# Four instead of two key tiles of the value product in parts, in five of eight chunks

## The chip, the cores and the metric

One core of a Trainium2 chip. The metric is the device time of one launch in microseconds (us), from the median of several runs. TensorE (PE) multiplies; VectorE (DVE), ScalarE (ACT) and GpSimd (POOL) work on vectors; SyncE (SP) issues the DMAs.

## What is computed

A transformer layer in fp32 on x of 4 x 1024 tokens x 256:

```
xn  = layernorm(x)
out = x + attention(xn) + ffn(xn)
attention: qkv = xn @ w_qkv, 16 heads of 128, rotary on q and k,
           softmax(q k^T / sqrt(128)) v, then @ w_out
ffn:       gelu(xn @ up + up_bias) @ down + down_bias, up and down in MXFP4 (blocks of 32)
```

## The kernel before

**Two ways to multiply fp32.** A product of plain fp32 operands is one call in the program and two matmul records in the trace. A product "in parts" splits both operands into a high part, rounded to the reduced type fp32r, and a low part (the value less its high part), and adds three reduced products: high x high, low x high, high x low. All products of the kernel are in parts, but for the value product (probabilities x v), which takes only the first two of its eight key tiles in parts (`SPLIT = 2`); the other six are plain fp32.

**Order of the work.** The 4 x 16 heads are taken as 32 pairs of heads. A pair has 8 chunks of 256 queries, 4 for each head; chunk number k mod 8 is called chunk 0 to 7 here. Each engine runs a function `step` once for each chunk, always in the same order, and the engines meet by semaphores. Two pairs are one round of 16 steps. The steps are in hardware loops whose body starts with step 4 of a round and ends with step 3 of the next (`PEELED = 4`), so that each engine jumps back between a step 3 and a step 4 in every second pair. The first eight pairs also split the projection weights.

**PE**, step k: scores of the next chunk's first 128 queries (`next_scores(0)`, L1222, into `s_ps`), a projection group of the next pair into `slot_ps`, scores of its second 128 queries, output projection of chunk k-2 (L1222, into `w_ps`), a second projection group, and last the value product of chunk k-1 (`values`, L1282 to L1306): L1296, L1297 and L1300 are the three products of each of the two tiles in parts, L1304 the six plain tiles. It waits for `p_hi_ready` ahead of L1296 and for `p_lo_ready` ahead of L1300.

At steps 3 and 7, `next_scores(0)` starts a new head, and waits first until all four rotated pieces of that head's q and k are there (`qk_ready`, L1273).

**DVE**, step k: transposes (L943) of the probabilities, from which the DMAs (L420) build `keys_first`, the probabilities with keys on the partitions; low part of the attention output (L963), row maxima (L933), output added to y (L974), and MXFP4 pieces.

**ACT**, step k: high part of the attention output of chunk k-2 (`high_out`, L767), copies of the projection groups out of PSUM (`take_group`; L722 for v, L735 to L737 for q and k), two exponentials (L755), the high part of a rotated piece (`rotated_high`, L747), and last the high part of the chunk's own probabilities (`probs_high`, L761): 128x512 elements of `keys_first` into `p_hi`, once its DMAs have landed.

**POOL**, step k, in this order: the low part of the probabilities of chunk k-1 (`probs_low`, L605, waits for L761), then the rotary work. A rotation (`rotated_sum`) is three operations, L584, L585 and L587. ACT then takes the high part (L747), and POOL the low part (`rotated_low`, L598), which raises `qk_ready`. The q and k pieces of the next pair's first head ("qk0", pieces 0 to 3) are rotated in steps 3, 4, 5 and 6; the low parts of pieces 0 and 1 come in steps 4 and 5 ahead of the next rotation, those of pieces 2 and 3 in step 6, around the last rotation. Those of the second head are rotated in steps 7, 0, 0 and 1. Step 0 is the one with two rotations.

In ACT's step k, `rotated_high` stands ahead of `probs_high`, and waits for POOL's rotation of the same step (in step 6 it stands ahead of the second exponential too).

The v projection comes in four groups of two key tiles; `V_TILES = (1, 2, 0, 3)` says which pair of tiles each holds. Only the group with tiles 0 and 1 (`V_SPLIT`) is split: high part by ACT (L722, `v_hi`), low part by DVE (L957, `v_lo`). The others are copied by ACT to `v_rows`. PE may write the PSUM bank again when that is done (`bank_free`).

Of the kernel before, what the change touches and what calls it, by code (L numbers as in the profile page):

```python
# [8 lines left out]
F32 = mybir.dt.float32  # L9
F32R = mybir.dt.float32r  # L10
U32 = mybir.dt.uint32
ACT = mybir.ActivationFunctionType
ALU = mybir.AluOpType
# [4 lines left out]
HEADS, HEAD = 16, 128  # L18
FF = 1024
P = 128  # L20
TOK = BATCH * SEQ
TILES = TOK // P
BT = SEQ // P
# [20 lines left out]
LN_STEP = TILES // ROUNDS  # L44
MX_HALF = MX_COLS // 2

SPLIT = 2


def layer(nc, d):  # L50
# [7 lines left out]
    with ExitStack() as ctx:  # L58
        def sb(name, shape, dt=F32):
            return ctx.enter_context(nc.sbuf_tensor(name, shape, dt))  # L60

        def sem(name):
            return ctx.enter_context(nc.semaphore(name))

        def pb(name, shape):
# [18 lines left out]

        qk_hi, qk_lo = seq_parts[:, 1], seq_parts[:, 2]

        v_rows = sb("v_rows", [P, 2, BT - SPLIT, 2 * HEAD])
        v_hi = sb("v_hi", [P, 2, SPLIT, 2 * HEAD], F32R)
        p_hi = seq_parts[:, 3, 0].rearrange("p c s -> p (c s)")[:, 0:2 * SPLIT * CHUNK].rearrange(
            "p (s a j q) -> p s a j q", s=2, a=2 * QUADS, j=SPLIT)  # L90
# [9 lines left out]
        keys_first = sb("keys_first", [P, 2, 2 * QUADS, BT, QUAD], F32R)  # L100
# [75 lines left out]
        v_ready = sem("v_ready")  # L176
        v_lo_ready = sem("v_lo_ready")
        p_hi_ready = sem("p_hi_ready")
        p_lo_ready = sem("p_lo_ready")
        scores_ready = sem("scores_ready")  # L180
        max_ready = sem("max_ready")
        probs_ready = sem("probs_ready")
# [59 lines left out]

        V_TILES = (1, 2, 0, 3)
        V_SPLIT = tuple(n for n in range(4) if V_TILES[n] < SPLIT // 2)

        USED = {"qk0": 5, "v": 12, "qk1": 11}

# [13 lines left out]
        def qk_number(part, n):  # L261

            return n + (4 if part == "qk1" else 0)
# [312 lines left out]
        def _(pool):  # L576
# [23 lines left out]
            def probs_low(c, k):  # L600

                slot = k % 2
                pool.wait_ge(p_hi_ready, c + 1)
                low = keys_first[:, slot, :, 0:SPLIT, :]
                nc.gpsimd.tensor_tensor(low, low.bitcast(F32), p_hi[:, slot, :, :, :].bitcast(F32),  # L605
                                        ALU.subtract).then_inc(p_lo_ready, 1)

            def w_low(p, part):

# [87 lines left out]
        def _(act):  # L697
# [17 lines left out]
            def take_group(p, place, part, n, parity, bank, first=False):  # L715


                act.wait_ge(proj_ready, p * 12 + place + 1)
                if part == "v":
                    at = 2 * V_TILES[n]  # L720
                    rows = v_hi[:, parity, at:at + 2, :] if n in V_SPLIT else v_rows[:, parity, at - SPLIT:at - SPLIT + 2, :]
                    nc.scalar.activation(rows, bank.rearrange("p (a b) -> p a b", a=2), ACT.Copy).then_inc(v_ready, 1)  # L722
                    return
                m = qk_number(part, n)

                if first and m == 4:
                    act.wait_ge(first_qk_dve, 1)
                elif first and m == 5:
                    act.wait_ge(first_qk_dve, 3)
                elif not (first and m < 4):  # L730
                    act.wait_ge(qk_ready, p * 8 + m - 1)
                scale = SCALE if n // 2 == 1 else 1.0
                a, b = rope_slot(p, m)
                h = HEAD // 2
                nc.scalar.activation(a, bank, ACT.Copy, scale=scale)  # L735
                nc.scalar.activation(b[0:h], bank[h:P], ACT.Copy, scale=scale)
                nc.scalar.activation(b[h:P], bank[0:h], ACT.Copy, scale=scale).then_inc(rope_in, 1)  # L737
# [20 lines left out]
            def probs_high(i, k):  # L758

                act.wait_ge(keys_moved[k % 4], chunk_moves(i, k))  # L760
                nc.scalar.activation(p_hi[:, k % 2], keys_first[:, k % 2, :, 0:SPLIT, :].bitcast(F32),  # L761
                                     ACT.Copy).then_inc(p_hi_ready, 1)

            def high_out(c, slot):
# [453 lines left out]
        def _(pe):  # L1218
# [63 lines left out]
            def values(i, k, first):  # L1282

                c, p = i * 16 + k, i * 2 + k // 8
                pe.wait_ge(keys_moved[k % 4], chunk_moves(i, k))
                if not (first and k == 0):
                    pe.wait_ge(o_lo_ready, c)
                if k % 8 == 0:
                    pe.wait_ge(v_ready, p * 4 + 3)
                    pe.wait_ge(v_lo_ready, (p + 1) * len(V_SPLIT))  # L1290
                parity, head, slot = (k // 8) % 2, (k // 4) % 2, k % 2
                cols = slice(head * HEAD, (head + 1) * HEAD)
                out = o_ps[:, 0:CHUNK]
                pe.wait_ge(p_hi_ready, c + 1)
                for kt in range(SPLIT):
                    nc.tensor.matmul(out, v_hi[:, parity, kt, cols], p_hi[:, slot, :, kt, :], start=(kt == 0), stop=False)  # L1296
                    nc.tensor.matmul(out, v_lo[:, parity, kt, cols], p_hi[:, slot, :, kt, :], start=False, stop=False)  # L1297
                pe.wait_ge(p_lo_ready, c + 1)
                for kt in range(SPLIT):
                    nc.tensor.matmul(out, v_hi[:, parity, kt, cols], keys_first[:, slot, :, kt, :], start=False, stop=False)  # L1300
                if k % 8 == 0:
                    pe.wait_ge(v_ready, p * 4 + 4)
                for kt in range(SPLIT, BT):
                    last = nc.tensor.matmul(out, v_rows[:, parity, kt - SPLIT, cols], keys_first[:, slot, :, kt, :].bitcast(F32),  # L1304
                                            start=False, stop=(kt == BT - 1))
                last.then_inc(o_ready, 1)  # L1306

# [94 lines left out]
            def step(i, k, first, last):  # L1402
                c = i * 16 + k
                t = c * 2
                tail = last and k >= 16

                def next_scores(n):
                    if last and k == 15:
                        return
                    k2 = 2 * k + 2 + n  # L1410
                    pe.wait_ge(probs_ready, t + n + 1)
                    scores(k2, i * 2 + k2 // 16, k2 % 8 == 0 or (first and k2 == 4))

                def slot(n):
                    bank = slot_ps[:, n]
                    if (k, n) == LN_SLOT:
                        bank_free(i, k, n, first, last)
                        pe.wait_ge(ln_xn_ready, i + 3)
                        for m in range(CT * LN_STEP):
                            ins = nc.tensor.transpose(bank[:, m * P:(m + 1) * P],  # L1420
                                                      ln_xn[:, m % LN_STEP, (m // LN_STEP) * P:(m // LN_STEP + 1) * P], ident[:, :])
                        ins.then_inc(ln_turned, 1)
                        return
                    if (k, n) == MX_SLOT:
                        bank_free(i, k, n, first, last)
                        pe.wait_ge(mx_ready, i + 1)
                        for m in range(MX_STEP // P):
                            ins = nc.tensor.transpose(bank[:, m * P:(m + 1) * P], mx_q[:, m * P:(m + 1) * P], ident[:, :])
                        ins.then_inc(mx_turned_ready, 1)
                        return  # L1430
                    g = group_at(k, n, last)
                    if not g:
                        return
                    place, part, num, ahead = g
                    if first and k == 0:
                        if n == 0:
                            pe.wait_ge(v_ready, 1)
                        else:
                            pe.wait_ge(rope_in, 6)
                    else:  # L1440
                        bank_free(i, k, n, first, last)
                    if num == 0:
                        pe.wait_ge(w_ready[part], (i * 2 + ahead + 1) * 16)
                    if place < 2 and ahead == 2:
                        pe.wait_ge(x_ready[place], ((i + 1) // 4 + 1) * 32)
                    project(part, num, bank)

                if tail:
                    up(0, 0, k - 16)
                else:  # L1450
                    next_scores(0)
                    slot(0)
                    next_scores(1)
                if not (first and k < 2):
                    output(c - 2, (k - 2) % 16, i * 2 + (k - 2) // 8, first and k == 2)
                if not tail:
                    slot(1)
                if not (first and k == 0) and not (last and k == 17):
                    values(i, k - 1, first)
# [74 lines left out]
```

## Time and profile before

| | |
|---|---|
| Median of 3 runs | 2454.54 us (2453.13 to 2455.77) |
| The profiled execution | 2453.68 us |
| Its span, first to last instruction | 2451.9 us |
| Busy: PE, DVE, ACT, POOL | 2417.3, 1920.8, 1678.6, 1731.7 us |
| Mean granted TensorE clock | 0.999 |

A busy share is that of the whole span. Matmul records overlap: the time that one takes of the engine is the distance from its start to the next one's start, not its duration. In the tables a waiting instruction's idle time is named with what ended it.

### The profile page before, as it was taken

The numbers are of one execution on the slowest core, as the hardware profiler recorded it, in microseconds if no ns is written. First come the engines' busy times: TensorE is split into PE (matmuls) and PEld (weight loads), VectorE is DVE, ScalarE is ACT, GpSimd is POOL, SyncE is SP. The second block draws the span as 40 slices with busy tenths as digits, with TensorE's granted clock in tenths as the row PEclk, the third lists the DMA queues.
The fourth block names the chain that finished last, engine by engine and source line by source line (L and its number), as shares of the span: only waits on it lengthen the run. The fifth ranks groups of instructions, "written<-read, shape, count | busy, mean of one in ns | idle before, by whom it ended". The sixth has DMA issues, their size and how long they took to land. (4 is left out here: it accounts for less than half of the span.)

```text
span 2451.9 us, 42811 instructions
## 1 busy us (share of the span) xinstructions
PE 2417.3 (99%) x13168; PEld 2123.8 (87%) x13168; DVE 1920.8 (78%) x2671; ACT 1678.6 (68%) x3039; POOL 1731.7 (71%) x1358
## 2 busy tenths in 40 slices
PE   6999999999999999999999999999999999999999
PEld 5888888888888888888888888888888888888798
DVE  7878888787877877787787778778777877777776
ACT  7777777776776777676677767667776766777433
POOL 4778877777777777777677777777777777777331
PEclk9999999999999999999999999999999999999999
DMA  4666666667666656667666666667676666656832
GB/s 143 181 170 167 169 158 177 158 167 195 183 161 150 156 148 162 156 151 195 180 159 147 164 154 152 162 149 190 158 183 156 151 162 149 156 146 171 240 132 69
DMA packets 400878, 396.72 MB, mean 162 GB/s; under 512 B 38656, under 2 KB 383104, under 8 KB 400768
## 3 DMA queue, kind: packets, MB, share of 16 engines
q1 hardware_dynamic: 400768, 395.67, 62.9%
q14 instruction: 91, 0.75, 0.1%
q8 instruction: 19, 0.31, 0.1%
HBM read 91.43 MB, written 35.65 MB: 52 GB/s over the span
## 5 line engine op out<-in xcount | busy, mean ns | idle before, releaser
L933 DVE TENSOR_REDUCE neg_max<-s_ps 128x1 f32<-128x1024 f32 x512 | 621.1, 1219 | 289.1 <-PE s_ps L1222 288.2
L1222 PE MATMUL s_ps<-seq_parts 128*128 128x512 f32 x3072 | 826.3, 408 | 1.3 <-DVE seq_parts L1097 0.8
L755 ACT ACTIVATE probs<-s_ps,neg_max 128x1024 f32<-128x1024 f32 x512 | 571.1, 1115 | 369.0 <-DVE neg_max L933 365.3
L1304 PE MATMUL o_ps<-keys_first,v_rows 128*128 128x256 f32 x3072 | 706.5, 380 | 1.3 <-ACT v_rows L722 1.3
L943 DVE STREAM_TRANSPOSE turned_blocks<-probs 128x1024 f32<-128x1024 f32 x512 | 630.6, 1237 | 61.3 <-ACT probs L755 38.8
L1222 PEld LDWEIGHTS s_ps<-seq_parts 128*128 128x128 f32 x3072 | 571.5, 188 | 116.9 <-ACT probs L755 1.4
L1304 PEld LDWEIGHTS o_ps<-keys_first,v_rows 128*128 128x128 f32 x3072 | 566.3, 190 | 68.1 <-ACT v_rows L722 1.5
L605 POOL TENSOR_TENSOR keys_first<-keys_first,seq_parts 128x512 fp32r<-128x512 f32 x256 | 333.0, 1301 | 318.1 <-ACT seq_parts L761 318.0
L584 POOL TENSOR_TENSOR rope_a<-rope_a,cos 128x512 f32<-128x512 f32 x252 | 325.7, 1292 | 178.8 <-ACT rope_b L737 178.6
L598 POOL TENSOR_TENSOR seq_parts<-rope_a,seq_parts 128x512 fp32r<-128x512 f32 x252 | 360.2, 1430 | 92.8 <-ACT seq_parts L747 92.8
L1222 PE MATMUL slot_ps<-seq_parts,w_parts 128*128 128x512 f32 x1506 | 387.9, 393 | 0.0
L587 POOL TENSOR_TENSOR rope_a<-rope_a,rope_b 128x512 f32<-128x512 f32 x252 | 326.0, 1294 | 19.8
L585 POOL TENSOR_TENSOR rope_b<-rope_b,sin 128x512 f32<-128x512 f32 x252 | 326.7, 1297 | 0.0
L1222 PEld LDWEIGHTS slot_ps<-seq_parts,w_parts 128*128 128x128 f32 x1506 | 272.9, 189 | 51.7 <-ACT rope_b L737 0.5
L747 ACT ACTIVATE seq_parts<-rope_a 128x512 fp32r<-128x512 f32 x252 | 222.1, 881 | 80.4 <-POOL rope_a L587 79.9
L974 DVE SCALAR_TENSOR_TENSOR y<-w_ps,inv_sum,y 128x256 f32<-128x256 f32 x512 | 224.4, 480 | 33.5 <-DVE inv_sum L951 7.8
L767 ACT ACTIVATE o_hi<-o_ps 128x256 fp32r<-128x256 f32 x256 | 98.0, 383 | 165.5 <-PE o_ps L1304 141.9
L1222 PEld LDWEIGHTS slot_ps<-w_parts,seq_parts 128*128 128x128 f32 x1524 | 197.5, 189 | 9.1 <-issue 0.9
L1222 PE MATMUL slot_ps<-w_parts,seq_parts 128*128 128x256 f32 x1524 | 203.1, 283 | 0.5 <-ACT rope_b L737 0.5
L1222 PEld LDWEIGHTS w_ps<-wo_parts,o_hi 128*128 128x128 f32 x1024 | 175.1, 190 | 29.5 <-DVE o_lo L963 9.1
L1222 PE MATMUL w_ps<-wo_parts,o_hi 128*128 128x256 f32 x1024 | 194.3, 282 | 6.4 <-DVE o_lo L963 6.3
L761 ACT ACTIVATE seq_parts<-keys_first 128x512 fp32r<-128x512 f32 x256 | 159.7, 624 | 59.3 <-DMA keys_first<-turned_blocks 57.8
(118 smaller groups left out, 2606.8 us busy)
## 6 DMA issues: line engine op xcount, KB each, us to landing
keys_first<-turned_blocks SPq DMA_DIRECT2D x2048, 128.0 KB, 2.7
w_parts<-w_qkv_parts SPq DMA_DIRECT2D x72, 512.0 KB, 4.2
w_qkv_parts<-w_parts SPq DMA_DIRECT2D x24, 512.0 KB, 3.7
wo_parts<-w_out_parts SPq DMA_DIRECT2D x48, 256.0 KB, 3.2
seq_parts<-xnt_parts SPq DMA_DIRECT2D x16, 512.0 KB, 4.4
w_raw<-in_w_qkv SPq DMA_DIRECT2D x24, 256.0 KB, 4.1
seq_parts<-xnt_parts SPq DMA_DIRECT2D x6, 1024.0 KB, 8.3
y<-in_x SPq DMA_DIRECT2D x16, 256.0 KB, 3.2
```

The source lines that it names most:

```text
L584: nc.gpsimd.tensor_tensor(a, a, cos[:, cols], ALU.mult).then_inc(rope_mult, 1)
L585: nc.gpsimd.tensor_tensor(b, b, sin[:, cols], ALU.mult).then_inc(rope_mult, 1)
L587: nc.gpsimd.tensor_tensor(a, a, b, ALU.add).then_inc(rope_sum, 1)
L598: nc.gpsimd.tensor_tensor(lo, total, hi.bitcast(F32), ALU.subtract).then_inc(qk_ready, 1)
L605: nc.gpsimd.tensor_tensor(low, low.bitcast(F32), p_hi[:, slot, :, :, :].bitcast(F32), ALU.subtract).then_inc(p_lo_ready, 1)
L747: nc.scalar.activation(hi, total, ACT.Copy).then_inc(rope_hi, 1)
L755: nc.scalar.activation(probs[:, k2 % 4, :], s_ps[k2 % 2][:, :], ACT.Exp, bias=neg_max[:, col:col + 1], accum_out=row_sum[:, col:col + 1]). ...
L933: nc.vector.tensor_reduce(neg_max[:, k2 % 16:k2 % 16 + 1], s_ps[k2 % 2][:, :], AXX, ALU.max, negate=True).then_inc(max_ready, 1)
L943: nc.vector.transpose(turned_blocks[:, k % 2, n].rearrange("p b j q -> p j b q"), probs[:, (2 * k + n) % 4, :].rearrange("p (j b q) -> p j ...
L974: last = nc.vector.scalar_tensor_tensor(rows, w_ps[:, n * DIM:(n + 1) * DIM], inv_sum[:, col:col + 1], rows, ALU.mult, ALU.add)
L1222: ins = nc.tensor.matmul(out, w, m, start=(n == 0), stop=(n == len(terms) - 1))
L1304: last = nc.tensor.matmul(out, v_rows[:, parity, kt - SPLIT, cols], keys_first[:, slot, :, kt, :].bitcast(F32), start=False, stop=(kt == B ...
```

## The change

Chunks 2 to 6 of each pair (`WIDE`) take four key tiles in parts, the others two as before (`NARROW`). In a wide chunk ACT's L761 takes 128x1024 elements, POOL does a second subtraction of 128x512 behind the first (a semaphore of its own, `p_lo_back`), and PE does 12 products in parts and 4 plain tiles. PE waits for both low parts ahead of the first product that reads one. Of v, tiles 2 and 3 (group 0) are now kept both ways: ACT copies the group to `v_rows` and then rounds it into `v_hi`, DVE makes its `v_lo`, and PE may write the bank again only after that. The order of the steps is otherwise the same.

```
+NARROW, SPLIT = 2, 4
+WIDE = (2, 3, 4, 5, 6)
...
+        V_COPIED = tuple(n for n in range(4) if V_TILES[n] >= NARROW // 2)
+        FRONT, BACK = slice(0, NARROW), slice(NARROW, SPLIT)
...
 probs_low (POOL)
-                low = keys_first[:, slot, :, 0:SPLIT, :]
-                nc.gpsimd.tensor_tensor(low, low.bitcast(F32), p_hi[:, slot, :, :, :].bitcast(F32),
-                                        ALU.subtract).then_inc(p_lo_ready, 1)
+                low = keys_first[:, slot, :, FRONT, :]
+                nc.gpsimd.tensor_tensor(low, low.bitcast(F32), p_hi[:, slot, :, FRONT, :].bitcast(F32),
+                                        ALU.subtract).then_inc(p_lo_front, 1)
+                if k % 8 in WIDE:
+                    low = keys_first[:, slot, :, BACK, :]
+                    nc.gpsimd.tensor_tensor(low, low.bitcast(F32), p_hi[:, slot, :, BACK, :].bitcast(F32),
+                                            ALU.subtract).then_inc(p_lo_back, 1)
...
 take_group (ACT)
+                    tiles = bank.rearrange("p (a b) -> p a b", a=2)
+                    if n in V_COPIED:
+                        ins = nc.scalar.activation(v_rows[:, parity, at - NARROW:at - NARROW + 2, :], tiles, ACT.Copy)
+                    if n in V_SPLIT:
+                        ins = nc.scalar.activation(v_hi[:, parity, at:at + 2, :], tiles, ACT.Copy)
+                    ins.then_inc(v_ready, 1)
...
 probs_high (ACT)
+                tiles = slice(0, SPLIT if k % 8 in WIDE else NARROW)
+                nc.scalar.activation(p_hi[:, k % 2, :, tiles, :], keys_first[:, k % 2, :, tiles, :].bitcast(F32),
                                      ACT.Copy).then_inc(p_hi_ready, 1)
...
 values (PE)
+                wide = k % 8 in WIDE
+                tiles = SPLIT if wide else NARROW
-                for kt in range(SPLIT):
+                for kt in range(tiles):
                     (high x high and low x high)
-                pe.wait_ge(p_lo_ready, c + 1)
+                pe.wait_ge(p_lo_front, c + 1)
+                if wide:
+                    pe.wait_ge(p_lo_back, wide_chunks(p, k))
+                for kt in range(tiles):
                     (high x low)
...
+                for kt in range(tiles, BT):
                     (plain fp32)
```

## Rows read from the trace of the kernel before

**Rows 1.** The page: busy time of each engine (share).
```profile
PE 2417.3 (99%) x13168; PEld 2123.8 (87%) x13168; DVE 1920.8 (78%) x2671; ACT 1678.6 (68%) x3039; POOL 1731.7 (71%) x1358
```
**Rows 2.** Waits: waiting engine and line, releaser, total us, times, longest.
```profile
ACT seq_parts L747 <- POOL rope_a L587: 79.9, 64, 2.0
...
PE o_ps L1300 <- POOL keys_first L605: 3.8, 2, 3.1
```
**Rows 3.** Timeline, PE, 1317 to 1321 us: start, us, line, operands, count.
```profile
1317.13 0.28 PE L1296 MATMUL o_ps<-seq_parts,v_hi 128*128 128x256 f32 x1
...
1317.85 2.75 PE L1304 MATMUL o_ps<-keys_first,v_rows 128*128 128x256 f32 x12
1320.25 1.73 PE L1222 MATMUL s_ps<-seq_parts 128*128 128x512 f32 x6
```
**Rows 4.** Timeline, POOL, 1285 to 1323 us: steps 3 to 7 of one pair.
```profile
1287.06 1.29 POOL L584 TENSOR_TENSOR rope_a<-rope_a,cos 128x512 f32<-128x512 f32 x1 [1.12 <-ACT rope_b L737]
...
1298.32 1.30 POOL L587 TENSOR_TENSOR rope_a<-rope_a,rope_b 128x512 f32<-128x512 f32 x1
...
1306.84 1.29 POOL L587 TENSOR_TENSOR rope_a<-rope_a,rope_b 128x512 f32<-128x512 f32 x1
1310.55 1.29 POOL L605 TENSOR_TENSOR keys_first<-keys_first,seq_parts 128x512 fp32r<-128x512 f32 x1 [2.42 <-ACT seq_parts L761]
1311.80 1.30 POOL L598 TENSOR_TENSOR seq_parts<-rope_a,seq_parts 128x512 fp32r<-128x512 f32 x1
...
1315.69 1.29 POOL L587 TENSOR_TENSOR rope_a<-rope_a,rope_b 128x512 f32<-128x512 f32 x1
1317.72 1.28 POOL L598 TENSOR_TENSOR seq_parts<-rope_a,seq_parts 128x512 fp32r<-128x512 f32 x1 [0.74 <-ACT seq_parts L747]
...
1322.80 1.30 POOL L584 TENSOR_TENSOR rope_a<-rope_a,cos 128x512 f32<-128x512 f32 x1 [2.19 <-ACT rope_b L737]
```
**Rows 5.** Timeline, ACT, 1283 to 1318 us: steps 2 to 6 of the same pair.
```profile
1283.93 0.63 ACT L761 ACTIVATE seq_parts<-keys_first 128x512 fp32r<-128x512 f32 x1 [1.11 <-DMA keys_first<-turned_blocks]
...
1291.00 1.14 ACT L747 ACTIVATE seq_parts<-rope_a 128x512 fp32r<-128x512 f32 x1 [0.87 <-POOL rope_a L587]
...
1299.75 1.14 ACT L747 ACTIVATE seq_parts<-rope_a 128x512 fp32r<-128x512 f32 x1
1309.34 0.62 ACT L747 ACTIVATE seq_parts<-rope_a 128x512 fp32r<-128x512 f32 x1
...
1317.01 0.63 ACT L747 ACTIVATE seq_parts<-rope_a 128x512 fp32r<-128x512 f32 x1 [1.65 <-POOL rope_a L587]
```
**Rows 6.** Timeline, all engines, 1223 to 1249 us: a pair with the jump back.
```profile
1223.91 0.39 ACT L767 ACTIVATE o_hi<-o_ps 128x256 fp32r<-128x256 f32 x1 [2.75 <-issue]
...
1246.86 1.27 POOL L598 TENSOR_TENSOR seq_parts<-rope_a,seq_parts 128x512 fp32r<-128x512 f32 x1 [0.74 <-ACT seq_parts L747]
...
1248.97 0.81 PE L1222 MATMUL s_ps<-seq_parts 128*128 128x512 f32 x2
```
**Rows 7.** Groups by shape, ACT and DVE: count | busy us, mean ns.
```profile
L761 ACT ACTIVATE seq_parts<-keys_first 128x512 fp32r<-128x512 f32 x256 | 159.7, 624 | 59.3 <-DMA keys_first<-turned_blocks 57.8
L767 ACT ACTIVATE o_hi<-o_ps 128x256 fp32r<-128x256 f32 x256 | 98.0, 383 | 165.5 <-PE o_ps L1304 141.9 <-issue 22.9
L722 ACT ACTIVATE v_rows<-slot_ps 128x512 f32<-128x512 f32 x96 | 56.5, 590 | 0.0
L957 DVE TENSOR_TENSOR seq_parts<-slot_ps,v_hi 128x512 fp32r<-128x512 f32 x31 | 21.1, 681 | 0.0
```
**Rows 8.** Timeline, PE, 52 to 58 us, the start of the kernel.
```profile
52.30 0.50 PE L1300 MATMUL o_ps<-keys_first,v_hi 128*128 128x256 f32 x2 [3.13 <-POOL keys_first L605]
54.06 4.24 PE L1304 MATMUL o_ps<-keys_first,v_rows 128*128 128x256 f32 x12 [1.26 <-ACT v_rows L722]
57.95 3.08 PE L1222 MATMUL s_ps<-seq_parts 128*128 128x512 f32 x12
```
**Rows 9.** Stretches: us, busy and count of PE, PEld, DVE, ACT, POOL, clock.
```profile
55.00:56.00 1.00, 1.00 (x4) 0.74 (x3) 0.00 (x0) 0.98 (x3) 0.87 (x1) 0.50 0.10 33
```

More of the change, by code:

```diff
@@ L45 @@
 MX_HALF = MX_COLS // 2
-SPLIT = 2
+NARROW, SPLIT = 2, 4
+WIDE = (2, 3, 4, 5, 6)
 def layer(nc, d):
@@ L85, in layer @@
         qk_hi, qk_lo = seq_parts[:, 1], seq_parts[:, 2]
-        v_rows = sb("v_rows", [P, 2, BT - SPLIT, 2 * HEAD])
+        v_rows = sb("v_rows", [P, 2, BT - NARROW, 2 * HEAD])
         v_hi = sb("v_hi", [P, 2, SPLIT, 2 * HEAD], F32R)
@@ L178, in layer @@
         p_hi_ready = sem("p_hi_ready")
-        p_lo_ready = sem("p_lo_ready")
+        p_lo_front = sem("p_lo_front")
+        p_lo_back = sem("p_lo_back")
         scores_ready = sem("scores_ready")
@@ L244, in layer, with wide_chunks @@
         V_SPLIT = tuple(n for n in range(4) if V_TILES[n] < SPLIT // 2)
+        V_COPIED = tuple(n for n in range(4) if V_TILES[n] >= NARROW // 2)
+        FRONT, BACK = slice(0, NARROW), slice(NARROW, SPLIT)
+        def wide_chunks(p, k):
+            return p * len(WIDE) + WIDE.index(k % 8) + 1
         USED = {"qk0": 5, "v": 12, "qk1": 11}
@@ L720, in take_group @@
                     at = 2 * V_TILES[n]
-                    rows = v_hi[:, parity, at:at + 2, :] if n in V_SPLIT else v_rows[:, parity, at - SPLIT:at - SPLIT + 2, :]
-                    nc.scalar.activation(rows, bank.rearrange("p (a b) -> p a b", a=2), ACT.Copy).then_inc(v_ready, 1)
+                    tiles = bank.rearrange("p (a b) -> p a b", a=2)
[4 more added lines that the diff above has]
+                    ins.then_inc(v_ready, 1)
                     return
@@ L760, in probs_high @@
                 act.wait_ge(keys_moved[k % 4], chunk_moves(i, k))
-                nc.scalar.activation(p_hi[:, k % 2], keys_first[:, k % 2, :, 0:SPLIT, :].bitcast(F32),
+                tiles = slice(0, SPLIT if k % 8 in WIDE else NARROW)
+                nc.scalar.activation(p_hi[:, k % 2, :, tiles, :], keys_first[:, k % 2, :, tiles, :].bitcast(F32),
                                      ACT.Copy).then_inc(p_hi_ready, 1)
@@ L1294, in values @@
                 pe.wait_ge(p_hi_ready, c + 1)
-                for kt in range(SPLIT):
+                wide = k % 8 in WIDE
+                tiles = SPLIT if wide else NARROW
+                for kt in range(tiles):
                     nc.tensor.matmul(out, v_hi[:, parity, kt, cols], p_hi[:, slot, :, kt, :], start=(kt == 0), stop=False)
                     nc.tensor.matmul(out, v_lo[:, parity, kt, cols], p_hi[:, slot, :, kt, :], start=False, stop=False)
-                pe.wait_ge(p_lo_ready, c + 1)
-                for kt in range(SPLIT):
+                pe.wait_ge(p_lo_front, c + 1)
+                if wide:
+                    pe.wait_ge(p_lo_back, wide_chunks(p, k))
+                for kt in range(tiles):
                     nc.tensor.matmul(out, v_hi[:, parity, kt, cols], keys_first[:, slot, :, kt, :], start=False, stop=False)
@@ L1302, in values @@
                     pe.wait_ge(v_ready, p * 4 + 4)
-                for kt in range(SPLIT, BT):
-                    last = nc.tensor.matmul(out, v_rows[:, parity, kt - SPLIT, cols], keys_first[:, slot, :, kt, :].bitcast(F32),
+                for kt in range(tiles, BT):
+                    last = nc.tensor.matmul(out, v_rows[:, parity, kt - NARROW, cols], keys_first[:, slot, :, kt, :].bitcast(F32),
                                             start=False, stop=(kt == BT - 1))
@@ L1436, in slot @@
                         if n == 0:
-                            pe.wait_ge(v_ready, 1)
+                            pe.wait_ge(v_lo_ready, 1)
                         else:
```

## The prediction

> **What bounds the kernel now.** I read the page first, then the waits, then the timelines of one pair. The page shows TensorE busy for 2417.3 of 2451.9 us, the other engines at 68 to 78% [rows 1]. In the list of waits PE hardly appears: it waited for POOL's low probabilities twice in 256 chunks, for 3.8 us [rows 2]. So PE's instruction stream sets the time, and a saving on PE is worth its full size as long as nobody else becomes late.
>
> Whether somebody does can't be read from busy shares. The list shows ACT's L747 waiting for POOL's L587, 64 times and 79.9 us in all [rows 2], and the timeline POOL waiting for ACT in turn: L605 for L761, L598 for L747 [rows 4]. In steps 3 to 6 these waits form one chain that is serial: in every step ACT's L761 (high probabilities) releases POOL's L605, behind it on POOL stand L598 and the three operations of a rotation, the rotation's end (L587) releases ACT's L747, and right behind L747 stands the next L761 [rows 4, 5]. The chain ends in step 6 with the last L598, for which PE waits before it starts step 7 (the next pair's scores). In this pair that L598 ended at 1317.72 + 1.28 = 1319.00 and PE began step 7 at 1320.25 [rows 3, 4]: 1.25 us to spare. In a pair with the loop's jump back it ended at 1248.13, and PE began at 1248.97 [rows 6]: 0.84 us. This margin is what I hold the change against, since it lays work on exactly this chain, and POOL's second rotation (step 0) is not in it.
>
> **What PE gains.** Start to start, the two tiles in parts take from 1317.13 to 1317.85, 0.72 us for six products, or 0.36 for a tile. The six plain tiles take from 1317.85 to 1320.25, 2.40 us, or 0.40 a tile [rows 3]. So a tile moved from plain to parts saves 0.04 us, two tiles 0.08 in a wide chunk, and with 5 x 32 = 160 wide chunks 12.8 us if nothing else moves. Rounding of the starts (0.01 us) makes that 11 to 15.
>
> By the Trainium skill ("FP8 and Floating Point Precision", section TensorE Precision Notes) true fp32 takes four passes through the array, where the reduced kind takes one read. Three instead of four passes would save 0.12 us a tile, 38 us in all. The rows above show a plain tile at 3.3 times the price of one reduced product, not 4 times, so I keep to them.
>
> **What is laid on the chain.** Two prices. POOL's second subtraction has the shape of L605, which took 1.29 us with 1.25 from its start to the next operation's start [rows 4]: +1.25. No row shows ACT's L761 at 128x1024. L767 at 128x256 took 383 ns, L761 at 128x512 624 ns [rows 7]: 241 ns for 256 columns. So I take +0.48; the bounds are +0.24 (that step once) and +0.62 (a second whole L761).
>
> Walk for the pair at 1284 to 1320 us, each figure the shift against its time before:
> - Step 3: L761 of chunk 2 (start 1283.93) ends 0.48 later, at 1285.04. POOL does two subtractions from 1285.12 and is free at 1287.62. Before, the rotation began at 1287.06, after a wait of 1.12 for ACT [rows 4, 5]. That slack goes and the rotation is 0.56 late. L747 had waited 0.87 for it, so it is 0.56 late too, and L761 of chunk 3 ends 1.04 late.
> - Step 4: +1.25 on POOL, so L587 (ended 1299.62) is 2.29 late. L747 began at 1299.75, 0.13 after it: 2.19 late. L761 of chunk 4: 2.67 late.
> - Step 5: +1.25, so L587 (ended 1308.13) is 3.92 late and ends at 1312.05. L747 stood at 1309.34 behind an exponential, a slack of 1.2: 2.74 late. L761 of chunk 5: 3.22 late.
> - Step 6: +1.25, so L587, L747 (which had waited 1.65) and the last L598 are 4.47 late: 1319.00 becomes 1323.47.
>
> PE's step 7 then begins at about 1323.5 instead of 1320.25: 3.2 us late for this pair. The 4 x 0.08 us that PE has saved in steps 3 to 6 only lengthen its wait (to 3.6 us).
>
> The pair with the jump back, the same way: rotation of step 3 0.67 late, L761 of chunk 3 0.87 (it had 0.29 of slack against its DMAs), step 4 1.30 (ACT's 2.75 us after the jump [rows 6] come behind that L761, so its lateness is passed on), step 5 3.03, step 6 4.28. The last L598 ends at 1252.41 instead of 1248.13, PE begins 3.5 us late. Some 0.9 us of this may be lost earlier, at step 4's output projection, whose operand comes after the jump; it is the same lateness, not more.
>
> After step 7 POOL and ACT are late by 4.3 to 4.5, PE by 3.2 to 3.5. POOL's next work waited 2.19 us for ACT before (its rotation at 1322.80) [rows 4], and PE-driven work is late by PE's figure only, so the difference is used up in step 7 and steps 0 to 2, all narrow, run as before. I take each pair to start fresh.
>
> **The v tiles.** ACT's added copy is 0.59 us, DVE's added low part 0.68 [rows 7], in step 5 of each pair. ACT there ends up waiting for POOL's L587 (1312.05 against 1309.34 before), which covers 0.59. DVE's stands ahead of the row maxima of step 5; they are then some 1.3 us late, and the exponentials behind them still end ahead of L587. Without the chain's lateness both would eat ACT's slack of 1.2. At the start of the kernel, where PE waits for ACT and POOL anyhow [rows 8], I add both: 1.3 us. The new wait for the low part ahead of a bank's reuse in step 5 ends some 0.7 us before PE gets there. Before step 7 it would anyway be part of the same lateness. PE's values themselves never wait: `p_lo` of chunks 2 to 6 is used half a step later.
>
> **The sum.** The chain exists in 31 pairs (the last has no next one): 16 even ones at 3.5 and 15 odd ones at 3.2 give 104. Chunk 6 in step 7 is behind the wait and gives its 0.08: -2.5. The last pair gains 0.4. The start costs 1.3. I take the eight weight-splitting pairs at the same price: their extra POOL work stands where POOL waits for L761. Together +102 us on the profiled 2453.7: 2556. The median of the runs shown is 0.9 above that execution: **2557 us**.
>
> With 0.24 for ACT's growth the chain is 1.0 shorter in each pair (four wide L761s), 31 in all: 2526. With 0.62 it is 0.6 longer: 2574. Ten falls of the clock (below) would add 15. Own range of the likeliest case: 2515 to 2590.
>
> **Rivals.**
> - *The clock falls in the new pause.* At 49 to 54 us PE had waits of 3.13 and 1.26 with 0.5 us of work between; then the granted clock was 0.50, the lower level of 1.2 GHz [rows 9], and 12 records that take 2.40 us took from 54.06 to 57.95, 3.89 [rows 8, 3]: 1.5 us lost. My pause is 3.6 us in one piece, so it could go the same way each time: 31 x 1.5 = 46 more, 2603. Against it: it is shorter than that pair of waits together. By the Trainium skill ("TensorE: Matmul & The Clock Gate", section Why this matters for your kernels) a pause of about this length between bursts is what to avoid. I give it 0.15; a few falls belong to the likeliest case.
> - *Faster: the chain isn't binding.* If ACT's high probabilities or POOL's subtraction overlap more than the timeline lets me see, so that the added 7 us on the chain come down to the 3.5 or so of slack and margin in it, then PE's 12.8 us show: 2453.7 - 12.8 + 1.3 + 0.9, 2443. It decides at the last L598 before PE's step 7. For it: the list of waits shows nothing of PE there now. Against: the chain is serial in the rows, with margins of 0.84 and 1.25. 0.08.
> - *Half of it:* the order of waits adjusts (the jump's 2.75 us shrink when ACT comes late, POOL's operations run closer while DVE is quieter), and the lateness is 1.5 a pair: 2453.7 + 47, about 2500. 0.12.
> - *The lateness does not start fresh:* steps 0 and 1 have two rotations, and what is left over makes PE wait there again; 1 us a pair more: 2588. 0.05, inside the range.
>
> **The numbers.** The forecast has 0.60, the rivals 0.15, 0.08, 0.12 and 0.05. Slower by over 0.2% (some 5 us, what can be told from no change) are all but the second: 0.90; to the faster case I give 0.08, to no change 0.02. The range goes from the half case to the clock's: 2500 to 2610.
>
> **What would show it.** In the profile after: PE waiting for POOL's L598 counterpart some 31 times by 2.5 to 3.6 us, at step 7 alone; PE's busy time little changed; wide value products 0.08 us shorter start to start; ACT's wide copy at about 1.1 us, the second subtraction at 1.29; ACT's waits for the rotations grown from 79.9 us to well over 200. Wrong, if PE's waits stay as short as now, or fall elsewhere (row maxima, the output projection, the bank in step 5), or if the clock row shows tenths missing in many slices.

## The result and the profile after

The changed kernel takes **2584.0 us** (median of 4 runs, 2581.05 to 2586.32) against 2454.9 before: ratio 1.0525, 95% interval 1.0511 to 1.0538. That is 129 us slower, where 102 were forecast; it lies inside the range.

The page after, busy time and mean granted clock in slices (line numbers are now those of the changed kernel: L1241 for L1222, L1317/L1318/L1323/L1327 for the value product, L615 and L619 for the two subtractions, L608 for the low parts of q and k, L597 for the rotation's end, L765 and L780 for ACT's high parts):

```profile
span 2584.5 us, 43910 instructions
PE 2456.4 (95%) x13488; PEld 2158.7 (84%) x13488; DVE 1959.0 (76%) x2703; ACT 1753.6 (68%) x3071; POOL 1929.8 (75%) x1518
```

PE is no longer busy throughout [rows 1]. Its waits, all of the list that are over 2 us, and ACT's for the rotations:

```profile
ACT seq_parts L765 <- POOL rope_a L597: 202.7, 121, 4.1
...
PE s_ps L1241 <- POOL seq_parts L608: 93.1, 31, 3.4
...
PE s_ps L1393 <- DVE probs L1025: 11.6, 1, 11.6
...
PE w_ps L1241 <- DVE o_lo L982: 7.9, 6, 3.3
...
PE o_ps L1323 <- POOL keys_first L615: 3.1, 1, 3.1
```

The new wait is the forecast one: 31 times, 3.0 us on average, scores that wait for POOL's last low part. ACT waits 202.7 us for rotations instead of 79.9 [rows 2].

One pair (odd, like the one of [rows 3 to 5]) on PE, end of step 6 and start of step 7:

```profile
1388.28 0.64 PE L1323 MATMUL o_ps<-keys_first,v_hi 128*128 128x256 f32 x4
1388.75 1.89 PE L1327 MATMUL o_ps<-keys_first,v_rows 128*128 128x256 f32 x8
1393.68 2.90 PE L1241 MATMUL s_ps<-seq_parts 128*128 128x512 f32 x6 [3.04 <-POOL seq_parts L608]
1396.38 1.75 PE L1241 MATMUL slot_ps<-w_parts,seq_parts 128*128 128x256 f32 x12
```

The six scores products at the start of step 7 now take from 1393.68 to 1396.38, 2.70 us. Before, the same six took from 1320.25 to 1321.82, 1.57 us, in the trace that [rows 3] come from:

```profile
1320.25 1.73 PE L1222 MATMUL s_ps<-seq_parts 128*128 128x512 f32 x6
1321.82 1.60 PE L1222 MATMUL slot_ps<-w_parts,seq_parts 128*128 128x256 f32 x12
```

The clock row of the stretch after says why (us, PE busy and count, granted clock, DMA share, GB/s):

```profile
1392.00:1393.00 1.00, 0.00 (x0) 1.00 0.83 165
1393.00:1394.00 1.00, 0.32 (x1) 0.67 0.82 210
1394.00:1395.00 1.00, 1.00 (x3) 0.50 0.58 142
1395.00:1396.00 1.00, 1.00 (x4) 0.50 0.12 19
1396.00:1397.00 1.00, 1.00 (x6) 0.63 0.86 172
1397.00:1398.00 1.00, 1.00 (x11) 1.00 0.87 216
```

At the end of the pause the clock falls to 0.50, the lower level of 1.2 GHz, and comes back while PE works. The granted clock fell around 29 of the 31 pauses. The mean over the execution is 0.975, against 0.999.

POOL in steps 3 to 6 of that pair, and ACT's part of the chain:

```profile
1358.10 1.31 POOL L594 TENSOR_TENSOR rope_a<-rope_a,cos 128x512 f32<-128x512 f32 x1
...
1364.23 1.30 POOL L615 TENSOR_TENSOR keys_first<-keys_first,seq_parts 128x512 fp32r<-128x512 f32 x1 [2.20 <-ACT seq_parts L780]
1365.48 1.30 POOL L619 TENSOR_TENSOR keys_first<-keys_first,seq_parts 128x512 fp32r<-128x512 f32 x1
...
1374.32 1.29 POOL L615 TENSOR_TENSOR keys_first<-keys_first,seq_parts 128x512 fp32r<-128x512 f32 x1 [2.20 <-ACT seq_parts L780]
...
1383.91 1.30 POOL L615 TENSOR_TENSOR keys_first<-keys_first,seq_parts 128x512 fp32r<-128x512 f32 x1 [1.69 <-ACT seq_parts L780]
...
1390.27 1.26 POOL L597 TENSOR_TENSOR rope_a<-rope_a,rope_b 128x512 f32<-128x512 f32 x1
1392.27 1.26 POOL L608 TENSOR_TENSOR seq_parts<-rope_a,seq_parts 128x512 fp32r<-128x512 f32 x1 [0.74 <-ACT seq_parts L765]
```
```profile
1382.26 0.63 ACT L765 ACTIVATE seq_parts<-rope_a 128x512 fp32r<-128x512 f32 x1 [0.74 <-POOL rope_a L597]
1382.79 1.04 ACT L780 ACTIVATE seq_parts<-keys_first 128x1024 fp32r<-128x1024 f32 x1
...
1391.56 0.63 ACT L765 ACTIVATE seq_parts<-rope_a 128x512 fp32r<-128x512 f32 x1 [4.14 <-POOL rope_a L597]
```

From the first L594 of step 3 to the end of the last L608 it is 35.43 us (1358.10 to 1393.53). In [rows 4] it was 31.94 (1287.06 to 1319.00). The walk had 4.47 - 0.56 = 3.91 for the difference, the trace says 3.49. From step 6's first subtraction to that end: 9.62 against 8.45, so 1.17 for the forecast 1.25.

### The profile page after: what moved, and what is told of

It reads as the page before. It is cut to its first block and busy times, and to the rows that moved or that the text cites. A ratio compares the mean times of both kernels' runs of the same rounds, so it can differ in the third digit from the quotient of the medians.

```text
span 2584.5 us, 43910 instructions
## 1 busy us (share of the span) xinstructions
PE 2456.4 (95%) x13488; PEld 2158.7 (84%) x13488; DVE 1959.0 (76%) x2703; ACT 1753.6 (68%) x3071; POOL 1929.8 (75%) x1518
## 5 line engine op out<-in xcount | busy, mean ns | idle before, releaser
L1241 PE MATMUL s_ps<-seq_parts 128*128 128x512 f32 x3072 | 856.1, 419 | 95.1 <-POOL seq_parts L608 93.1
L1241 PEld LDWEIGHTS s_ps<-seq_parts 128*128 128x128 f32 x3072 | 588.9, 195 | 226.3 <-ACT probs L773 106.6
L615 POOL TENSOR_TENSOR keys_first<-keys_first,seq_parts 128x512 fp32r<-128x512 f32 x256 | 331.6, 1296 | 372.4 <-ACT seq_parts L780 371.8
L1327 PE MATMUL o_ps<-keys_first,v_rows 128*128 128x256 f32 x2432 | 569.2, 380 | 1.0 <-ACT v_rows L737 1.0
L1327 PEld LDWEIGHTS o_ps<-keys_first,v_rows 128*128 128x128 f32 x2432 | 445.2, 191 | 51.6 <-ACT v_rows L737 1.3
L608 POOL TENSOR_TENSOR seq_parts<-rope_a,seq_parts 128x512 fp32r<-128x512 f32 x252 | 359.7, 1428 | 80.8 <-ACT seq_parts L765 80.8
L1241 PE MATMUL slot_ps<-seq_parts,w_parts 128*128 128x512 f32 x1506 | 388.1, 393 | 0.0
L594 POOL TENSOR_TENSOR rope_a<-rope_a,cos 128x512 f32<-128x512 f32 x252 | 325.3, 1291 | 70.4 <-ACT rope_b L755 68.5
L765 ACT ACTIVATE seq_parts<-rope_a 128x512 fp32r<-128x512 f32 x252 | 222.3, 882 | 202.9 <-POOL rope_a L597 202.7
L597 POOL TENSOR_TENSOR rope_a<-rope_a,rope_b 128x512 f32<-128x512 f32 x252 | 327.3, 1299 | 19.8
L1241 PEld LDWEIGHTS slot_ps<-seq_parts,w_parts 128*128 128x128 f32 x1506 | 272.8, 189 | 51.9 <-ACT rope_b L755 0.5
L780 ACT ACTIVATE seq_parts<-keys_first 128x1024 fp32r<-128x1024 f32 (+1 forms) x256 | 227.2, 888 | 60.0 <-DMA keys_first<-turned_blocks 60.0
L1241 PEld LDWEIGHTS slot_ps<-w_parts,seq_parts 128*128 128x128 f32 x1524 | 219.3, 209 | 11.8 <-ACT rope_b L755 0.5
L1241 PE MATMUL slot_ps<-w_parts,seq_parts 128*128 128x256 f32 x1524 | 221.5, 299 | 0.3 <-ACT rope_b L755 0.3
L1317 PE MATMUL o_ps<-seq_parts,v_hi 128*128 128x256 f32 x832 | 214.0, 287 | 0.0
L1318 PE MATMUL o_ps<-seq_parts 128*128 128x256 f32 x832 | 212.3, 285 | 0.0
L619 POOL TENSOR_TENSOR keys_first<-keys_first,seq_parts 128x512 fp32r<-128x512 f32 x160 | 206.9, 1293 | 0.0
```

What stands on the lines that cost most here:

```text
L594: nc.gpsimd.tensor_tensor(a, a, cos[:, cols], ALU.mult).then_inc(rope_mult, 1)
L597: nc.gpsimd.tensor_tensor(a, a, b, ALU.add).then_inc(rope_sum, 1)
L608: nc.gpsimd.tensor_tensor(lo, total, hi.bitcast(F32), ALU.subtract).then_inc(qk_ready, 1)
L780: nc.scalar.activation(p_hi[:, k % 2, :, tiles, :], keys_first[:, k % 2, :, tiles, :].bitcast(F32), ACT.Copy).then_inc(p_hi_ready, 1)
L1241: ins = nc.tensor.matmul(out, w, m, start=(n == 0), stop=(n == len(terms) - 1))
L1327: last = nc.tensor.matmul(out, v_rows[:, parity, kt - NARROW, cols], keys_first[:, slot, :, kt, :].bitcast(F32), start=False, stop=(kt == ...
```

## The experiments

Every kernel is the changed one with the edit shown, except where said. Times are medians, each compared with runs of the kernel before on the same chip (2454.9 to 2456.0).

**e1: ACT's high probabilities ahead of the rotation's high part.**

```
 ACT step, k % 8 in (3, 4, 5):
+    probs_high(i, k)
     rotated_high(p + 1, "qk0", k % 8 - 3)
-    probs_high(i, k)
```

> The changed kernel with one order swapped on ACT: in steps 3, 4 and 5 the wide high probabilities (probs_high) come ahead of the rotation's high part (rotated_high), so that POOL's two subtractions no longer wait for L765 of the same step. All work is kept. Theory (the serial chain of POOL and ACT in steps 3 to 6 is the whole loss, its clock falls included): a step of the chain is then 2.5 + 1.4 + 3.9 = 7.8 us, under every step's 8.0 to 9.6, so PE's 31 waits of 3.0 at step 7 go (under 5 us in all), and with them the clock falls; PE's saving shows, which in the trace after is 0.14 us in each of 160 wide chunks: 2454.9 - 22 + 1 = about 2434. Rival (POOL's added amount of work, 207 us, wherever it stands): within 10 us of 2584.

Measured: 2492.5 us (ratio 1.0155, 1.0138 to 1.0172). With all its work kept the kernel is 92 us faster than the changed one, so the rival (amount of work) falls; but 58 us are missing to the theory's 2434. Its trace:

```profile
PE s_ps L1245 <- POOL seq_parts L608: 41.0, 31, 2.6
```
```profile
1405.38 1.28 POOL L597 TENSOR_TENSOR rope_a<-rope_a,rope_b 128x512 f32<-128x512 f32 x1
1408.00 1.30 POOL L615 TENSOR_TENSOR keys_first<-keys_first,seq_parts 128x512 fp32r<-128x512 f32 x1 [1.34 <-ACT seq_parts L780]
1409.26 1.29 POOL L619 TENSOR_TENSOR keys_first<-keys_first,seq_parts 128x512 fp32r<-128x512 f32 x1
...
1416.39 1.26 POOL L608 TENSOR_TENSOR seq_parts<-rope_a,seq_parts 128x512 fp32r<-128x512 f32 x1 [0.74 <-ACT seq_parts L765]
```

PE still waits: 1.3 us a pair on average, up to 2.6 in the early pairs, where the clock still fell twice. The list counts a wait from the modelled end of the last matmul. From start to start, step 6 is 52 us longer in sum than in e5, which accounts for most of the 58. In the pair shown POOL is idle for 1.34 us ahead of step 6's subtractions, because ACT reaches L780 only after its second exponential, and step 6 itself is no shorter: 9.65 us from 1408.00 to 1417.65. The theory had counted POOL's own work and forgotten that L780 also has a place in ACT's queue.

**e2: no second subtraction.**

```
 probs_low (POOL):
-                if k % 8 in WIDE:
-                    ... low parts of tiles 2 and 3, p_lo_back
 values (PE):
-                if wide:
-                    pe.wait_ge(p_lo_back, wide_chunks(p, k))
```

> The changed kernel without POOL's second subtraction and PE's wait for it; tiles 2 and 3 of the wide chunks are multiplied as they are in the place of their low part, so this part of the product is left out. ACT's wide copy (0.42 us longer) and PE's products stay. Theory: the chain is 0.4 to 0.9 late at the last low part of step 6, which the margin of 1.25 covers in odd pairs, and that of 0.84 not quite in even ones, where PE's earlier arrival (0.56) is waited away: about 2443, PE waiting under 15 us at step 7, no clock falls. Rival (ACT's growth is what makes the chain late): above 2500, with most of the 31 waits still over 1.5 us.

Measured: 2443.9 us (0.9955, 0.9939 to 0.9972), PE waiting for L608 9 times and 3.9 us in all. Both as expected. ACT's 0.42 us a chunk by themselves fit into the margin; with POOL's 1.25 they don't. (POOL's without ACT's was not run.)

**e3: PE as before, ACT and POOL as changed.**

```
 values (PE):
-                tiles = SPLIT if wide else NARROW
+                tiles = NARROW
```

> The changed kernel, but PE multiplies every chunk as before (two tiles in parts, six plain ones, the plain ones reading what the second subtraction left in tiles 2 and 3, so the product is not the reference's). ACT and POOL do all they do in the changed kernel. Theory (time is set by the chain, PE's saving is waited away in steps 3 to 6): only chunk 6's 0.14 x 32 = 4.5 us come on top; the waits at step 7 shrink by 4 x 0.14 to about 2.4 us, and with that some of the 29 clock falls go (the two pairs of the changed kernel that waited 2.2 us had none), up to 1.6 us each: 2555 to 2588. Rival (PE's stream still counts everywhere): 2584 + 22 = 2606.

Measured: 2569.8 us (1.0467, 1.0449 to 1.0484). Taking all of PE's saving away makes the kernel 14 us *faster*. The waits are 74.3 us in all, 2.4 each, and the clock falls at 19 of the 31 instead of 29 (mean clock 0.985 instead of 0.975). The rival, 2606, is out: on this chain PE's speed isn't what the time hangs on.

**e4: idle products ahead of the wait.**

```
 scores (PE):
                 if tile_ready:
+                    if head == 0 and k2 > 4:
+                        for n in range(8):
+                            nc.tensor.matmul(s_ps[k2 % 2][:, 0:HALF], qk_hi[:, 1, 0, 0:P],
+                                             qk_hi[:, 1, 1, 0:HALF], start=True, stop=True)
                     pe.wait_ge(qk_ready, ...)
```

> The changed kernel with eight idle products of 128x512 (1.9 us) on PE ahead of its wait at step 7, into the bank that the scores then overwrite. Nothing else moves. Theory (the clock's falls are a cost of their own, 29 in 31 pairs, 1.5 to 1.9 us each, on top of the waits): the recorded wait shrinks to about 1.1 us, the granted clock stays at 1.00, and the time falls by 29 x 1.55 = 45, to about 2539. Rival (the falls cost nothing, because what PE loses it would wait for anyway): within 5 us of 2584. If the added products outlast the wait: slower than 2584.

Measured: 2565.5 us (1.0453, 1.0436 to 1.0471): 18 us faster than the changed kernel, where 45 were expected. The clock stays up (mean 0.998), and the products after the wait run at full speed again (1381.97 to 1383.46, 1.49 us for six):

```profile
1378.28 2.20 PE L1294 MATMUL s_ps<-seq_parts 128*128 128x512 f32 x8
1381.97 1.66 PE L1241 MATMUL s_ps<-seq_parts 128*128 128x512 f32 x6 [1.49 <-POOL seq_parts L608]
1383.46 1.59 PE L1241 MATMUL slot_ps<-w_parts,seq_parts 128*128 128x256 f32 x12
```
```profile
PE s_ps L1241 <- POOL seq_parts L608: 34.3, 29, 1.6
PE s_ps L1241 <- issue: 14.5, 14, 1.4
```

Summed over the trace, from start to start, steps 6 and 7 are 46 us shorter than in the changed kernel: the theory's amount. But 14 new waits of PE of some 1 us each came in, which the list puts down to nothing but issue. They stand ahead of step 4's first scores, behind the loop's jump, at each of the loop's 14 jumps back, and the steps that hold them are 19 us longer in sum. So the falls cost what the theory says, and the kernel of e4 lost nearly half of it again, most of that at the jump. Why is open: this run also put more products into PE's loop, and e10 below bears on that.

**e5: e1, and on POOL the last rotation of step 6 ahead of the subtractions.**

```
 POOL step:
+                if k8 == 6 and more_pairs:
+                    rotated_sum(p + 1, "qk0", 3)
                 if not (first and k == 0):
                     probs_low(c - 1, k - 1)
 ...
                 if k8 == 6 and more_pairs:
                     rotated_low(p + 1, "qk0", 2)
-                    rotated_sum(p + 1, "qk0", 3)
                     rotated_low(p + 1, "qk0", 3)
```

> The kernel of e1 (high probabilities ahead of the rotation's high part on ACT in steps 3 to 5), and on POOL in step 6 the last rotation (piece 3) put ahead of the two subtractions. All five chunks wide, all work kept. In e1 POOL stood idle for 1.34 us ahead of step 6's subtractions, with the last rotation's input there, and PE still waited 1.2 us at step 7. Theory (order, not amount of work, makes the chain late): the last low part ends some 2 us earlier than in e1, PE's waits at step 7 under 5 us in all, PE's saving shows: 2454.9 - 22 + 1 = 2434, up to 2440 if the weight-splitting pairs still wait. Rival (ACT's and POOL's larger load in steps 3 to 6 keeps about a microsecond a pair): 2480 to 2495 as in e1. If the subtractions now come too late for PE's products of chunk 5: waits at L1327 for POOL, 1 us a pair.

Measured: **2436.2 us** (0.9927, 0.9913 to 0.9941), as expected, and faster than both kernels. All of the change's work is in it. Its trace shows no wait of PE for L608 at all, and POOL without a pause between two rotations and two subtractions:

```profile
span 2435.7 us, 43882 instructions
PE 2400.9 (99%) x13488; PEld 2121.3 (87%) x13488; DVE 1974.6 (81%) x2703; ACT 1749.9 (72%) x3071; POOL 1931.2 (79%) x1518
```
```profile
1371.49 1.27 POOL L597 TENSOR_TENSOR rope_a<-rope_a,rope_b 128x512 f32<-128x512 f32 x1
1372.71 1.29 POOL L594 TENSOR_TENSOR rope_a<-rope_a,cos 128x512 f32<-128x512 f32 x1
...
1376.61 1.29 POOL L615 TENSOR_TENSOR keys_first<-keys_first,seq_parts 128x512 fp32r<-128x512 f32 x1
1377.86 1.29 POOL L619 TENSOR_TENSOR keys_first<-keys_first,seq_parts 128x512 fp32r<-128x512 f32 x1
```

POOL and ACT are as busy in microseconds as in the changed kernel (1931.2 and 1749.9 against 1929.8 and 1753.6). Only the order differs, by 148 us.

**e6: e1 with chunk 5 narrow.**

```
-WIDE = (2, 3, 4, 5, 6)
+WIDE = (2, 3, 4, 6)
```

> The kernel of e1 with chunks 2, 3, 4 and 6 wide, chunk 5 as before: one subtraction (1.25 us) and 0.42 us of ACT less in step 6, the last of the chain. Theory: e1's wait of 1.2 us at step 7 goes in most pairs; 4 x 32 x 0.14 = 18 saved: 2454.9 - 18 + 1 = 2438, to 2444 with what the weight-splitting pairs (2.3 us in e1) still wait. Rival (what is left in e1 comes from ACT's load, the v copies of 0.59 us in step 5): waits stay at 1 us, 2475.

Measured: 2445.8 us (0.9960, 0.9946 to 0.9974); PE waits for L608 5 times, 2.8 us in all. The wait went as expected. The time is 2 us above the expected band's upper end and 8 over the value; Against e5's trace, whose time is itself 2 us over its expected value, step 6 is 8.9 us longer in sum: 4.3 are chunk 5's saving, which is not made here, and the remaining 4.6 lie at PE's wait, mostly in the early pairs. So most of e1's remaining wait came from chunk 5, in the last step of the chain: its second subtraction and ACT's 0.42 us, which this run takes out together.

**e7: chunk 6 alone wide; e8: no chunk wide (the v tiles alone).**

```
-WIDE = (2, 3, 4, 5, 6)
+WIDE = (6,)        (e7)
+WIDE = ()          (e8)
```

> The changed kernel with chunk 6 alone wide: its longer copy on ACT and its second subtraction come after the last rotation's high part and at the start of step 7, behind the point where PE waits. The v tiles are kept both ways as in the changed kernel. Theory (place on the chain decides): no waits at step 7, 32 x 0.14 = 4.5 saved, v's copies at 0 to 1.3 us: 2451 to 2452. Rival (any wide chunk costs its 1.7 us of POOL and ACT): 2454.9 + 31 x 1.0 or more, above 2480.

> The changed kernel with no wide chunk: what is left is the second copy of v's group 0 (ACT 0.59 us), its low part on DVE (0.68 us) and PE's wait for it at the bank's next use, once in each pair. Theory: all hidden but for the start, 0 to 1.3 us: 2455 to 2456.5. Rival (they eat the slack of 1.2 us before L747 in step 5 and make the chain late by themselves): 2460 to 2475.

Measured: e7 2450.9 us (0.9981, 0.9972 to 0.9990), e8 2456.6 (1.0002, 0.9993 to 1.0011). A wide chunk that lies behind PE's wait costs nothing and brings 5.7 us against e8, 0.18 in each of 32 (between the two traces step 7 differs by 0.14 on average). The v copies are hidden.

**e9: the kernel before with e5's two orders.**

```
 probs_high ahead of rotated_high (ACT, steps 3 to 5); rotated_sum(.., 3) ahead of probs_low (POOL, step 6)
```

> The kernel before with e5's two orders and nothing else (two tiles in parts everywhere). Theory: the chain had a margin of 0.84 to 1.25 us there, so a shorter chain brings nothing: within 2 us of 2455, and e5's gain is PE's saving. Rival (the orders are themselves faster, hidden waits elsewhere): 2445 or less.

Measured: 2456.5 us (1.0003, 0.9993 to 1.0012). The orders alone bring nothing: e5's 19 us are PE's saving.

**e10: e5 with chunk 7 wide too.**

```
-WIDE = (2, 3, 4, 5, 6)
+WIDE = (2, 3, 4, 5, 6, 7)
```

> The kernel of e5 with chunk 7 wide as well (six of eight). Its subtractions stand at the start of POOL's step 0, ahead of a low part and two rotations. Theory (only slack on POOL's chain counts): PE saves 32 x 0.14 = 4.5 more, but POOL's two rotations of step 0 and the low probabilities of chunks 0 and 1 behind them come 1.25 us later; the latter had 0.6 to 1.0 us to spare at L1300 in the kernel before, less its wait for ACT of 0.5, so PE waits up to 0.5 us in half of the pairs: 2432 to 2442. Rival (POOL's step 0 is full, so the whole 1.7 us are lost in each pair): 2436 + 50 = 2485.

Measured: 2464.6 us (1.0034, 1.0021 to 1.0046), 28 slower than e5: between the two expectations, and both had the wrong place. PE's wait for the low probabilities did not grow:

```profile
PE s_ps L1246 <- issue: 16.3, 14, 1.7
...
PE o_ps L1328 <- POOL keys_first L615: 3.8, 2, 3.1
```

What grew is again the wait behind the loop's jump, at each of the 14 jumps; the steps that hold them are 21 us longer in sum than in e5. My reading was that PE, held at step 3 by the second head's low parts (L608), can't run ahead across the jump and then shows the jump's own cost. The trace doesn't bear it out:

```profile
1359.57 1.28 POOL L608 TENSOR_TENSOR seq_parts<-rope_a,seq_parts 128x512 fp32r<-128x512 f32 x1 [0.88 <-ACT seq_parts L766]
1362.89 3.12 PE L1246 MATMUL s_ps<-seq_parts 128*128 128x512 f32 x12
1372.25 1.65 PE L1246 MATMUL s_ps<-seq_parts 128*128 128x512 f32 x6 [0.98 <-issue]
```

The last L608 ended 2.04 us before step 3 began here, and 1.4 to 2.0 in the other pairs with the jump from pair 8 on; in e5, without such waits, it was 1.5 to 1.7. What e10 and e4 have in common is the length of PE's loop. Their traces hold 13552 and 13736 matmul records, every other run's 13488 or fewer, and these two alone show waits at the jump: at all 14 of them. In e3, with fewer products in the loop, the pause at 1536.27 (2.53 us) passed without a fall of the clock, and no wait stands behind the next jump; that one case speaks against a pause at full clock as the cause. The length is therefore the likelier cause. That is not shown: no run changes the length of the loop and nothing else.

## Why the prediction was right, and where it was off

**What bounds the kernel, and the chain.** Right. The forecast stood on a margin of 0.84 to 1.25 us at one wait, and PE now waits at that place 31 times, for 2.2 to 3.4 us, and nowhere else anew. e2 (subtraction gone, 2444), e5 (order changed, 2436) and e3 (PE's saving gone, 2570) show that it is the chain and not the amount of work or PE.

**What PE gains: mis-sized.** The prediction said 0.08 us a wide chunk, from 0.40 for a plain tile. A wide chunk's product takes from 1401.45, its first record, to 1404.43, the next scores:

```profile
1401.45 0.28 PE L1317 MATMUL o_ps<-seq_parts,v_hi 128*128 128x256 f32 x1
...
1402.89 1.89 PE L1327 MATMUL o_ps<-keys_first,v_rows 128*128 128x256 f32 x8
1404.43 0.81 PE L1241 MATMUL s_ps<-seq_parts 128*128 128x512 f32 x2
```

That is 2.98 against 3.12 in [rows 3], 0.14 less. The four plain tiles take 1.54 and six took 2.40, so the one more or less costs 0.43, not the mean of 0.40: each group is some 0.18 shorter than its tiles at that price. With 0.36 for a tile in parts a tile saves 0.07. e5 against before bears it out: 160 x 0.14 = 22 less some 1 to 3 at the start. The Trainium skill's rule of four passes for true fp32 ("FP8 and Floating Point Precision", TensorE Precision Notes), which I had put aside for the mean, would have erred on the other side: 0.43 us are 3.6 of the reduced products' 0.12, between the mean's 3.3 and four, and the saving of 0.07 a tile lies between my 0.04 and the 0.12 by that rule. It didn't move the forecast much, since in four of five wide chunks the saving is waited away.

**What is laid on the chain.** POOL's +1.25 was exact. ACT's 128x1024 copy takes 1.05 us, not 1.11:

```profile
L780 ACT ACTIVATE seq_parts<-keys_first 128x1024 fp32r<-128x1024 f32 x160 | 167.9, 1049 | 54.8 <-DMA keys_first<-turned_blocks 54.8
```

So +0.42 instead of +0.48. From the first scores' starts of pairs 8 to 30 in both traces, steps 3 to 5 are 0.43 shorter in sum, step 6 is 3.3 longer: PE starts step 7 about 2.9 us late, where the walk had 3.2 and 3.5. 31 x 2.9 = 90 us; the prediction had 104.

**The clock: the step that failed.** The rival had 0.15, "a few falls belong to the likeliest case", since my pause was "shorter than that pair of waits together" [rows 8]. The clock fell at 29 of 31 pauses. In pairs 8 to 30 step 7 is 1.5 us longer than before, its saving of 0.14 already in; over the whole trace, with the two early pairs without a fall, it is 43 us. 90 + 43 is 133, and the two profiled executions differ by 132.6 (the medians by 129). So the forecast put a term at nothing that measured a third of the loss. The sign named for it, tenths missing in the clock row, couldn't show it: the page prints a 9 for everything from 0.90 up, so 0.975 looks there like 0.999. The mean and the rows of single microseconds show it. The Trainium skill's warning of such pauses ("TensorE: Matmul & The Clock Gate", Why this matters for your kernels) holds here: the trace agrees, with a recorded wait of 3.0 us. The rival's own sum (2603) erred on the other side, because it was set on top of 3.2 to 3.5. What happened is this rival, which had a chance of 0.15, and not the likeliest case with 0.60: 2584 lies 27 above the forecast and 19 below the rival. That the forecast came this near is in part luck, since 14 us too many on the chain hid a part of the clock's.

**"I take each pair to start fresh."** Right: steps 0 to 2 together differ from before by under 2 us in the whole trace. In e4, where the clock stays up, they are 2 us longer than that; what e4 lost again it lost behind the jump.

**The v tiles, PE's own waits.** Right: e8 is within its error of before, and L1323 waited for POOL once.

**The faster rival** (2443) names what the change could have brought. It needed the chain out of the way, which took two changes of order, not luck in the overlap: e5.

## What to carry to other kernels

Where one engine is busy 99% of the time and others 70%, look for the last release of each of its waits and how much earlier than needed it came, before laying work on an idle-looking engine: here 1.0 us of margin stood against 6.7 us of work on a serial chain. Work that isn't urgent (these subtractions were due half a step later) belongs behind the urgent in an in-order queue, and that order is cheap to change. A pause of some 3 us on TensorE cost more than itself here, 1.5 us more each, and the price of removing a product is read from two group sizes, not from a mean. An experiment that adds instructions to a loop can change something else than what it is meant for: look for waits at new places before reading its time as the price of the thing tested.

## What the runs showed of the hardware

- In the changed kernel all 28 recorded waits of 2.7 to 3.4 us went with a fall to half the clock, and one of the three of 2.2. In e3 it was 19 of 28 waits of 2.3 to 3.0 and none of three of 1.6; in e1 two of five of 2.3 to 2.6, and none of the 26 of 0.8 to 1.3.
- Two plain fp32 tiles more (128x256) cost 0.86 us, six products in parts 0.72.
- PE showed waits of 0.7 to 1.7 us behind each of the loop's 14 jumps in e4 and e10, the two runs with the most matmul records, and none there in any other run.
